# Decoder layer, first pass: z products and copies at units 27 to 49, two x products at units 12 and 14

## The reference, cut to what is computed

```python
xz = jnp.einsum('bld,ed->ble', x, in_proj_w)
xc, z = jnp.split(xz, 2, axis=-1)            # 512 channels each
xs = jax.nn.silu(conv1d_causal(xc, conv_w) + conv_b)
dt, Bm, Cm = jnp.split(xs @ x_proj_w.T, [64, 80], axis=-1)
dt = jax.nn.softplus(dt @ dt_proj_w.T + dt_proj_b)
# for each of 16 states n:  h = exp(dt * A[:, n]) * h + dt * Bm[n] * xs;   y += Cm[n] * h
y = (y + D * xs) * jax.nn.silu(z)
x = layernorm(x + y @ out_proj_w.T)
```

## Time and profile before

| | us |
|---|---|
| median of 3 runs | 7266.84 (7264.4 to 7272.13) |
| the profiled execution's own time | 7281.31 |
| its span | 7279.5 |
| PE busy | 6712.2 (92%) |
| DVE busy | 5405.5 (74%) |
| ACT busy | 4456.3 (61%) |
| POOL busy | 4589.0 (63%) |

### The profile page before, as it was taken

The page is one execution under the profiler, slowest core; times in us unless marked ns, Lnnn a source line. Parts: engine busy times, 40 slices in busy tenths (PEclk is TensorE's granted clock), DMA queues, the critical chain, the costliest instruction groups (busy, mean ns, idle before and its releaser), DMA issues. The chain is left out here.

```text
span 7279.5 us, 106079 instructions
## 1 busy us (share of the span) xinstructions
PE 6712.2 (92%) x24272; PEld 3702.6 (51%) x24272; DVE 5405.5 (74%) x13962; ACT 4456.3 (61%) x9788; POOL 4589.0 (63%) x3991
## 2 busy tenths in 40 slices
PE   2899999999999999999999999997789999999997
PEld 1354444544445444454445544454656666666664
DVE  5588888888888888888888888887436666666665
ACT  2778888788877888878888788885212112221111
POOL 0788888888888888888888888897011112111111
PEclk6999999999999999999999999998889999999998
DMA  1666556665666666666556655566611111111110
GB/s 42 137 142 151 140 144 156 154 146 144 143 150 153 147 144 143 152 153 149 143 135 151 158 147 144 137 151 176 208 35 33 32 32 32 32 32 32 32 32 20
DMA packets 554199, 834.94 MB, mean 115 GB/s; under 512 B 169180, under 2 KB 207389, under 8 KB 551713
## 3 DMA queue, kind: packets, MB, share of 16 engines
q1 hardware_dynamic: 552768, 820.23, 46.1%
q10 hardware_dynamic: 864, 8.65, 0.3%
HBM read 745.91 MB, written 74.45 MB: 113 GB/s over the span
## 5 line engine op out<-in xcount | busy, mean ns | idle before, releaser
L1250 POOL TENSOR_TENSOR arena<-arena 128x512 f32<-128x512 f32 x2048 | 2581.9, 1276 | 276.4 <-DVE arena L1175 249.2
L875 PE MATMUL psum<-arena 128*128 128x512 f32 x4096 | 2192.3, 632 | 43.7 <-POOL arena L1250 37.9
L1175 DVE TENSOR_TENSOR_SCAN arena<-arena,psum 128x512 f32<-128x512 f32 x1024 | 1237.2, 1208 | 385.4 <-ACT arena L1044 297.9
L1263 POOL TENSOR_TENSOR arena<-arena 128x512 f32<-128x512 f32 x1024 | 1331.6, 1300 | 149.8 <-PE psum L875 149.5
L1031 ACT ACTIVATE arena<-arena 128x128 f32<-128x128 f32 x4096 | 1304.8, 396 | 134.0 <-PE psum L860 133.6
L1179 DVE TENSOR_TENSOR_SCAN arena<-psum,arena 128x512 f32<-128x512 f32 x1024 | 1234.8, 1206 | 87.4 <-ACT psum L1044 26.0
L875 PEld LDWEIGHTS psum<-arena 128*128 128x128 f32 x4096 | 712.0, 199 | 599.0 <-issue 385.4
L1044 ACT ACTIVATE arena<-arena 128x508 f32<-128x508 f32 x1024 | 738.5, 721 | 57.8 <-DVE arena L1175 57.1
L1829 POOL TENSOR_SCALAR arena<-arena 128x4 f32<-128x4 f32 x160 | 37.0, 231 | 1164.9 <-DVE arena L1690 1164.9
L860 PEld LDWEIGHTS psum<-arena 128*128 128x128 f32 x4096 | 518.7, 146 | 489.2 <-issue 441.4
L1044 ACT ACTIVATE psum<-arena 128x508 f32<-128x508 f32 x1024 | 701.5, 685 | 64.8 <-DVE arena L1179 31.0
(11 more groups left out here) (218 smaller groups left out, 10103.8 us busy)
## 6 DMA issues: line engine op xcount, KB each, us to landing
arena<-bc_scratch SPq DMA_DIRECT2D x1152, 512.0 KB, 5.3
arena<-in_xT_dram SPq DMA_DIRECT2D x32, 512.0 KB
arena<-in_x_dram SPq DMA_DIRECT2D x32, 512.0 KB, 7.8
x_scratch<-arena SPq DMA_DIRECT2D x32, 512.0 KB, 5.7
xin_scratch<-arena SPq DMA_DIRECT2D x128, 128.0 KB, 2.5
arena<-kernel_scratch SPq DMA_DIRECT2D x32, 512.0 KB, 7.0
arena<-x_scratch SPq DMA_DIRECT2D x32, 512.0 KB, 3.8
out_dram<-arena SPq DMA_DIRECT2D x32, 512.0 KB
```

The costliest lines, as they stand in the source:

```text
L875: pe.matmul(y_ps, ident, ring[:, u % RING], start=False, stop=n == NS - 1).then_inc(S["nsum"], 1)
L1175: dve.tensor_tensor_scan(s, decay_sb[:, u // 2 % 2], bx_ps[:, u // 2 % 2], 0.0, ALU.mult, ALU.add)\
L1250: pool.tensor_tensor(h, h, Cb[:, u // 2 % PAIRS, u % 2], ALU.mult).then_inc(S["hc"], 1)
L1263: pool.tensor_tensor(ring[:, u % RING], uu[par][:, c], Bb[:, state(u)], ALU.mult)\
```

## The change

The z products move on PE from units 13, 13, 14, 19 to 27, 32, 38, 47, and their ACT copies from 12, 14, 15, 19 to 29, 34, 40, 49. Silu of z is a step of its own (`sz`), at ACT's unit 24 behind `si`, and works on the z of the block that is running, not of the next one. The x products xc2 and xc3 move on PE from units 6 and 7 to 12 and 14, on ACT from 6 and 9 to 13 and 15, on DVE from 5 and 6 to 14 and 16. POOL's first gate moves from unit 20 to 28. The load of xT moves from pair 12 to pair 26, since z3 now reads xT at unit 47. The banks change with PE_AT's order: x1T's two tiles now follow xc2 and xc3 in their banks, xc2 and xc3 follow the out projection's tiles, and z2 follows the first `at` tile.

```diff
--- before.py
+++ after.py
@@ -54,7 +54,7 @@
 PAIRS = 4
 BC_AT = 15
 Y_AT = 2
-GATE_AT = 4
+GATES = {28: 0, 36: 1, 52: 2}
 NEG = -3.0e38
 OFF = -1.0e30
 
@@ -86,22 +86,14 @@
 )
 
 
-FRONT = ["xc0", "xc1", "xc2", "xc3", "z0", "z1", "z2", "z3", "si", "xp", "bt", "dt0", "dt1", "dt2", "dt3",
-         "se", "sr", "sl", "ds0", "ds1", "ds2", "ds3", "sp0", "sp1", "sp2", "sp3", "tu0", "tu1", "tu2", "tu3"]
+FRONT = ["xc0", "xc1", "xc2", "xc3", "si", "xp", "bt", "dt0", "dt1", "dt2", "dt3",
+         "se", "sr", "sl", "z0", "z1", "z2", "z3", "ds0", "ds1", "ds2", "ds3", "sp0", "sp1", "sp2", "sp3", "tu0", "tu1", "tu2", "tu3"]
 BACK = (["y3", "op0", "op1", "op2", "op3", "ln1", "mask", "rs1", "x1", "ln2", "rs2", "x1T", "qk"]
         + [s + str(b) for b in range(G) for s in ("sc", "tka", "tkb", "tkc", "tkd", "sm", "dg", "at")]
         + ["xa", "film0", "film1", "film2", "film3"])
-PE_AT = dict(xc0=2, xc1=3, xc2=6, xc3=7, op0=8, op1=8, op2=9, op3=10, z0=13, z1=13, z2=14, x1T=17, z3=19, qk=21,
-             sc0=22, xp=24, bt=26, dt0=29, sc1=29, dt1=30, dt2=34, at0=35, dt3=36, sc2=36, at1=40, ds0=42, ds1=43,
-             ds2=44, sc3=45, at2=49, ds3=51, tu0=53, at3=53, xa=54, tu1=55, film0=56, film1=58, tu2=59, film2=60,
-             tu3=60, film3=62)
-ACT_AT = dict(xc0=5, y3=5, xc1=5, xc2=6, xc3=9, z0=12, x1=14, z1=14, z2=15, x1T=16, z3=19, qk=23, si=24, xp=26,
-              sm0=26, bt=28, dt0=31, dg0=31, dt1=33, dt2=34, sm1=36, dt3=38, at0=39, se=39, dg1=39, sl=40, at1=42,
-              sm2=44, ds0=44, ds1=46, dg2=46, ds2=48, at2=49, sm3=50, ds3=52, dg3=52, at3=53, tu0=53, xa=54, tu1=56,
-              tu2=62, tu3=63)
-DVE_AT = dict(xc0=4, xc1=4, xc2=5, xc3=6, ln1=12, ln2=18, tka0=24, tkb0=24, tkc0=24, tkd0=26, sm0=26, tka1=31,
-              tkb1=32, tkc1=33, tkd1=34, sm1=35, tka2=38, sr=38, tkb2=39, tkc2=40, tkd2=41, sm2=42, tka3=46, tkb3=47,
-              tkc3=48, tkd3=49, sm3=49, film0=57, film1=59, film2=62, film3=63)
+PE_AT = dict(xc0=2, xc1=3, op0=8, op1=8, op2=9, op3=10, xc2=12, xc3=14, x1T=17, qk=21, sc0=22, xp=24, bt=26, z0=27, dt0=29, sc1=29, dt1=30, z1=32, dt2=34, at0=35, dt3=36, sc2=36, z2=38, at1=40, ds0=42, ds1=43, ds2=44, sc3=45, z3=47, at2=49, ds3=51, tu0=53, at3=53, xa=54, tu1=55, film0=56, film1=58, tu2=59, film2=60, tu3=60, film3=62)
+ACT_AT = dict(xc0=5, y3=5, xc1=5, xc2=13, x1=14, xc3=15, x1T=16, qk=23, si=24, sz=24, xp=26, sm0=26, bt=28, z0=29, dt0=31, dg0=31, dt1=33, z1=34, dt2=34, sm1=36, dt3=38, at0=39, se=39, dg1=39, z2=40, sl=40, at1=42, sm2=44, ds0=44, ds1=46, dg2=46, ds2=48, z3=49, at2=49, sm3=50, ds3=52, dg3=52, at3=53, tu0=53, xa=54, tu1=56, tu2=62, tu3=63)
+DVE_AT = dict(xc0=4, xc1=4, ln1=12, xc2=14, xc3=16, ln2=18, tka0=24, tkb0=24, tkc0=24, tkd0=26, sm0=26, tka1=31, tkb1=32, tkc1=33, tkd1=34, sm1=35, tka2=38, sr=38, tkb2=39, tkc2=40, tkd2=41, sm2=42, tka3=46, tkb3=47, tkc3=48, tkd3=49, sm3=49, film0=57, film1=59, film2=62, film3=63)
 POOL_AT = dict(mask=4, y3=6, rs1=15, rs2=21, sp0=45, sp1=48, sp2=53, sp3=59)
 
 
@@ -666,7 +658,7 @@
                         load_b(i, 3)
                     if v == 10 and back:
                         store_x1(i - 1)
-                    if v == 12 and ahead:
+                    if v == 26 and ahead:
                         need(sp, "in_mm", i + 1, 8)
                         load_xT(i + 2)
                     if v == 16:
@@ -926,6 +918,7 @@
                 elif name == "si":
                     need(act, "conv", i, C)
                     act.activation(xs[par], xs[par], ACT.Silu).then_inc(S["xs"], 1)
+                elif name == "sz":
                     need(act, "zc", i, C)
                     act.activation(zs[par], zs[par], ACT.Silu).then_inc(S["zs"], 1)
                 elif name == "xp":
@@ -1033,7 +1026,7 @@
                 a.then_inc(S["bxt"], 1)
 
             def iteration(i, par, front, back):
-                names = which_steps(front, back)
+                names = which_steps(front, back) + ["sz"]
                 for u in range(C * NS):
                     c, n, k = u // NS, u % NS, state(u)
                     if n == 0:
@@ -1052,7 +1045,9 @@
                     if u > NS and n == Y_AT:
                         read_y(i, c - 1)
                     for s in steps_at(ACT_AT, u, names):
-                        if s in FRONT:
+                        if s == "sz":
+                            step(s, i, par)
+                        elif s in FRONT:
                             step(s, i + 1, 1 - par)
                         else:
                             step(s, i - 1, 1 - par)
@@ -1264,8 +1259,8 @@
                             .then_inc(S["bx"], 1)
                     if u >= POOL_LAG or back:
                         times_c(i, u - POOL_LAG)
-                    if u > NS and u % NS == GATE_AT:
-                        gate(i, par, u // NS - 1)
+                    if u in GATES:
+                        gate(i, par, GATES[u])
                     for s in steps_at(POOL_AT, u, names):
                         if s in FRONT:
                             step(s, i + 1, 1 - par)
```

## The result

| | median of runs, us | ratio to before, with its 95% interval | profiled execution: time, mean granted clock |
|---|---|---|---|
| before, in the same series | 7265.6 | | 7281.3, 0.947 |
| after | 7330.5 | 1.0089 [1.0071, 1.0106] | 7331.9, 0.961 |

The changed kernel is 0.9% slower. The forecast said slower, 7292, range 7240 to 7345: right in sign and range, 38.5 us too low at the point. The pair of profiles differs by 50.6 us, the medians by 64.9, since the profiled execution of before lies over its median.

A forecast was written before the change was run, and what follows sets the result against it. The bound was taken as handed round a ring: PE in front, PE then ACT in the middle, POOL in the tail. Terms -3.6 + 3.44 + 0.96 + 0.1 = +0.9 us a block, 25 us over 28 blocks: 7292, range 7240 to 7345.

The forecast's parts named there:

- Middle, PE: z0 and z1 stand before the sum that the y copy of unit 34 needs: copy 3.44 us later per block.
- Middle, ACT: z1 and z2 copies (units 34, 40) fall where ACT has no gap, 0.48 each: 0.96 us more per block.
- Gate, sz, xT, z3 in the tail: POOL's first gate, z's Silu and the xT load cost nothing per block; z2 and z3 on PE together 0.1 us.
- Front, PE: Two x products leave units 6 and 7: PE's queue comes 3.44 us earlier, front gain 3.6 us per block.
- the wait for the convolution: Front, before the second half of x1T: PE waits over 2 us for DVE's convolution to free xc3's bank.
- Rival 1: Units 27 to 33: z0 and z1 keep the clock up, 1.2 GHz losses go, -48 us in all, 7244; chance 0.24.
- that +0.9: Sum of the forecast's terms per block: 0.9 us slower, bounds -3.6 and +2.
- signs of being wrong: Undisturbed block under 150; clock 1.00 in units 27 to 33 of all blocks; POOL waiting for a DMA in every block.
- 151: Sign of being right: undisturbed blocks last near 151 us.
- Rival 3: Front: PE's wait for the convolution before x1T brings a new clock drop, 1.5 us a block, 7334; chance 0.13.

The follow-up runs named there:

- experiment 3: Before with only POOL's first gate at unit 28 instead of 20 and the xT load at pair 26 instead of 12; 7258.9 us, 0.9999.
- experiment 9: Before with the gates and xT load of experiment 3, z3's product moved to unit 47, its copy to 49, Silu to the next block; 7267.9 us, 0.9997.
- experiment 10: The split with z3 alone moved from units 36 / 36 to 47 / 49 (product / copy); 7244.2 us, 0.9958.
- experiment 8: The split with z2 and z3 moved on PE from units 35 and 36 to 46 and 48, copies to 47 and 49; 7305.9 us, 1.0057.
- Experiment 1: After with x products xc2 and xc3 back at PE units 6 and 7 (ACT 6 and 9, DVE 5 and 6); 7333.9 us, 1.0109.
- experiment 11: After with xc3 at PE unit 12 and its copy at 13, ahead of x1, and both convolutions earlier (13 and 14); 7328.4 us, 1.0078.
- experiment 7: Before with ACT's z0, z1, z2 copies moved behind x1 (units 14, 15, 16) and PE's z2 from unit 14 to 15; 7264.3 us, 1.0001.
- The split: After with x products back at 6, 7, z0 and z1 at 13 copied behind x1, z2 and z3 at 35, 36; 7229.8 us, 0.9969; again 0.9965.
- experiment 5: After with z1's product moved from PE unit 32 to 36, behind the sum, and its ACT copy from 34 to 36; 7324.8 us, 1.0086.
- experiment 2: After with z0 and z1 on PE at units 35 and 36, behind the sum, and their copies there too; 7323.9 us, 1.0097.

## Why the prediction was right, and where it was off

**Middle, PE (+3.44 taken): right.** An undisturbed block has 27.5 with two z products ahead of the sum, 25.8 with one, 24.1 with none. PE had no slack there, as the step says.

**Middle, ACT (+0.96): right.** y to ds is 27.5, 28.0, 28.5 and 29.0 with none, one, two and three z copies there, in every kernel of the table.

**Gate, sz, xT, z3 in the tail (0 or 0.1): right** in time, by experiments 3, 9 and 10. Two products in the tail would not have been free (experiment 8).

**Front, PE (-3.6 taken): the failed step.** "The out projections, ln1 and the rest of PE's queue come 3.44 us earlier" took two products from PE as if PE were the bound at units 6 and 7. PE's timeline of after, block 13:

```profile
2213.36 1.13 PE L867 MATMUL psum<-arena 128*128 128x512 f32 x2 [1.02 <-POOL arena L1245]
...
2215.81 1.12 PE L867 MATMUL psum<-arena 128*128 128x512 f32 x2 [0.89 <-POOL arena L1245]
2216.77 3.62 PE L777 MATMUL psum<-arena 128*128 128x256 f32 x16
...
2227.99 1.88 PE L731 MATMUL psum<-arena 128*128 128x512 f32 x4
...
2239.87 0.66 PE L787 MATMUL psum<-arena 128*128 128x128 f32 x4 [2.68 <-DVE arena L1094]
```

PE catches up with POOL and waits 1.02 and 0.89 us for its products. The out projection starts 11.93 us behind the block's start instead of 12.87, so 0.94 earlier, and 2.5 of the 3.44 are lost. What follows went nearly as predicted, only later: the wait for the convolution came out at 2.68, and the second x1T product starts 35.0 us behind the block's start, where the prediction's times give 2211.7 - 2179.51 = 32.2. So k is 0.6 to 0.7 earlier in an undisturbed block and not 3.6; of the 3.0 that are missing, 2.5 are this step.

The trace of before already told it. Windows, POOL and PE of before, block 13 (start 2179.51):

```profile
2179.00:2191.00 12.00, 12.00 (x35) 5.67 (x34) 8.71 (x11) 6.75 (x15) 11.84 (x12) 1.00 0.98 249
...
2189.14 2.52 POOL L1250 TENSOR_TENSOR arena<-arena 128x512 f32<-128x512 f32 x2
...
2191.52 1.02 PE L875 MATMUL psum<-arena 128*128 128x512 f32 x2
2192.38 3.62 PE L785 MATMUL psum<-arena 128*128 128x256 f32 x16
```

POOL was as full as PE there, 11.84 of 12 us. The sum right ahead of the out projection starts at 2191.52, and the POOL product that it adds (the first of the two) ended at about 2190.4. So PE could win 1.1 us at that place, whatever left its queue.

Experiment 1 prices the x part in the changed kernel: with the x products back, k of an undisturbed block is at 44.4. Units 12 and 14 did not bring it forward, they cost 1.3 us; without the wait for the convolution, in experiment 11, k is at 44.1. What the front won came from the z products that left.

**The wait that went.** Taking away ACT's wait for z0, the largest in the earlier trace rows, was worth nothing by itself (experiment 7): x1 came 2.1 us earlier, then ACT stood 1.4 us for x1T on PE, and k came when it did before. The split differs from that kernel by z2 and z3 behind the sum and the parts of experiment 3, and has k at 44.0 instead of 46.3 in an undisturbed block. Some 0.3 of this is experiment 3's; the rest came with z2 and z3 gone from ahead of k.

**Rival 1: its mechanism happened, its place was right, and its price.** The stretches at 27 to 30 went from 14 blocks to 1, worth 1.6 us a block, 45 us; the rival said 48. The time that the rival gave, 7244, was wrong because it took over the forecast's front, and the missed front (2.6 x 28 = 73 us) outweighed it: -1.0 + 3.4 - 1.6 + 0.9 - 0.1 = +1.6 a block. The forecast put the clock at nothing, so it missed two terms, the front by +2.6 and the clock by -1.6. They are opposite in sign, and that +0.9 came as near to +1.6 as it did is partly luck. Of its signs of being wrong, the clock of 1.00 at units 27 to 33 did come up (27 of 28 blocks), and an undisturbed block lasts 153.3 us or more, not 151.

**Rival 3** hardly happened in after: 3 blocks have a stretch behind PE's wait for the convolution, all others have the wait and none. In its neighbours it did: with the x products back, 21 blocks got such a stretch, there behind PE's wait for POOL (2.16 us in block 5).

What stays open is why the stretches come where they do. All 298 that lie between Silu and y copy in the fourteen traces begin within 1.2 us of the end of a score product's eight matmuls with 32 rows. PE's timeline of experiment 11, ahead of its window from 877.5:

```profile
876.20 2.00 PE L816 MATMUL psum<-arena 32*128 32x128 f32 x8
```

But there are two such products in that part of every block, 784 in all, and most are followed by no stretch, in blocks 16 and 22 of experiment 11 neither; so the score product may be needed for one and is not enough. The stretches in the front (experiment 1) have no score product ahead of them. The sum of k and Silu to y is 73.4, 73.4, 73.3 and 73.4 in after and in experiments 1, 5 and 11 (2 has 72.9), though their undisturbed values run from 71.5 to 73.2. That each local gain over after was eaten by 1.2 GHz stretches is shown; that the sum comes out so nearly the same is not explained, and what in PE's work calls a stretch up was not tried by itself.

## What to carry to other kernels

Before you take an instruction's whole time as won for all that stands behind it in a queue, ask what else the queue is fed by at that very place: two products left PE, and it stood for POOL and won 0.9 us. The longest wait in the table may be worth nothing; take it away alone and look at the next event on the path, not at the waiting engine. And where a kernel's blocks come in a quick and a slow form, price an edit twice, in the undisturbed block and in how many blocks stay undisturbed; the second can cancel the first.

## What the runs showed of the hardware

TensorE ran at 1.2 GHz in stretches of 3.4, 6.8 or 10.2 us, and not only where PE idled: granted clock 0.57 with PE busy 4.00 of 4.00 us in experiment 1, and 0.59 with 3.94 of 4.00 in experiment 11. What PE did before differs. In experiment 1 it had stood 2.16 us for POOL. In block 14 of before it had been busy 7.57 of 8.00 us at clock 1.00, and then came 8.00 of 8.00 at 0.57:

```profile
2388.00:2396.00 8.00, 7.57 (x30) 3.64 (x29) 7.75 (x26) 7.97 (x23) 5.52 (x5) 1.00 0.52 136
```

A stretch of 3.4 us ahead of the y copy costs 1.6 us, one of 6.8 costs 3.3 (24.1, 25.7, 27.4 us from Silu to y copy in the split). The Trainium skill (TensorE: Matmul & The Clock Gate, Part 1) says that activity releases the throttle. Adding z0 and z1 at 27 and 32 did keep the clock at 1.00 there, which speaks for it; that a PE busy all of 4 us is granted 0.57 does not follow from it.

A copy of 128x512 from PSUM costs ACT 0.48 to 0.5 us in a dense stretch, start to start, less than its own 0.59. And a PSUM bank handed from an x product to the next product cost PE 4.03 us for DVE's convolution where the products themselves take 1.72.
